# Two transformer layers on 16 items: every engine's order written out, ring tiles chosen per item, fewer identity products

## The reference

```python
# layer 0
h = x + attention(rmsnorm(x), rmsnorm(x), sa_wq, sa_wk, sa_wv, sa_wo)   # 16 heads of 16
h = h + attention(rmsnorm(h), ctx, ca_wq, ca_wk, ca_wv, ca_wo)
h = h + (silu(rmsnorm(h) @ wg) * (rmsnorm(h) @ wu)) @ wd                # 1024 inner
# layer 1
nX, nF = layernorm(ctx, w1, b1), layernorm(h, w2, b2)
att = softmax(nF @ nX.T / 16) @ nX
cross = gelu(att @ fc1_w.T + fc1_b, approximate=False) @ fc2_w.T + fc2_b   # 4 inner
nc = layernorm(cross, w3, b3)
out = nF + gamma2 * (cross + gamma1 * softmax(nc @ nc.T / 16) @ nc)
```

## Time and profile before

| | us |
|---|---|
| median of 3 runs | 936.92 |
| lowest, highest | 936.81, 940.48 |
| the profiled execution: its span, by which it is timed | 938.1 |

### The profile page before, as it was taken

How to read it: one execution, slowest core, us unless ns; L and a number is a source line. 1 busy time by engine, 2 the same in 40 slices (tenths; PEclk the granted TensorE clock), 3 DMA queues, 4 the chain that set the end, 5 groups by cost and what they waited for, 6 DMA issues and landing times.

```text
span 938.1 us, 21220 instructions
## 1 busy us (share of the span) xinstructions
...
## 2 busy tenths in 40 slices
...
GB/s 207 191 148 128 134 76 81 61 105 26 57 101 43 94 64 80 79 81 56 102 38 55 104 44 95 63 81 77 80 55 92 50 43 105 43 33 35 17 12 23
...
## 3 DMA queue, kind: packets, MB, share of 16 engines
...
## 4 chain that ended last, share of the span: by engine, by line
PE 74%; DVE 12%; ACT 6%; issue 3%; DMA 2%; SPq 1%; POOL 1%; ACTq 0%; DVEq 0%
PE mring L1527 21%; PE ring L1527 12%; PE down_ps L1667 9%; PE od L1634 9%; PE ring L1620 7%; PE ring L1600 6%; DVE mx_sa L1296 4%; PE ring L1535 2%; PE mring L1696 1%; PE mring L1769 1%; DVE late_a L1343 1%; ACT probs L1094 1%; PE ring L1607 1%; PE mring L1677 1%; DMA pk_sa<-qkT 1%
## 5 line engine op out<-in xcount | busy, mean ns | idle before, releaser
L1094 ACT ACTIVATE probs<-ring 128x1024 f32<-128x1024 f32 (+1 forms) x192 | 190.9, 1022 | 45.3 <-PE ring L1620 41.5
L849 POOL TENSOR_TENSOR hidT_lo<-late_a,hidT_hi 128x256 fp32r<-128x256 f32 x128 | 95.8, 750 | 316.9 <-ACT hidT_hi L1121 315.7
L1296 DVE TENSOR_REDUCE mx_sa<-ring 128x4 f32<-128x1024 f32 x128 | 153.4, 1215 | 11.4 <-PE ring L1600 11.3
L1301 DVE TENSOR_REDUCE mx_ca<-ring 128x4 f32<-128x308 f32 x128 | 55.1, 474 | 59.8 <-PE ring L1600 59.7
L1349 DVE SCALAR_TENSOR_TENSOR late_a<-late_a,mring 128x256 f32<-128x256 f32 x128 | 52.9, 413 | 49.1 <-ACT late_a L1111 48.7
L1667 PE MATMUL down_ps<-down_hi,hidT_hi 128*128 128x256 f32 x256 | 79.0, 309 | 0.0
L1111 ACT ACTIVATE late_a<-mring 128x256 f32<-128x256 f32 x128 | 48.4, 378 | 51.2 <-PE mring L1527 48.9
L1600 PE MATMUL ring<-pk_sa 63*128 63x256 f32 x512 | 62.8, 329 | 14.9 <-DVE mx_sa L1296 6.4
L1667 PE MATMUL down_ps<-down_lo,hidT_hi 128*128 128x256 f32 x256 | 71.3, 279 | 0.0
L1667 PE MATMUL down_ps<-down_hi,hidT_lo 128*128 128x256 f32 x256 | 71.3, 279 | 0.0
L1121 ACT ACTIVATE hidT_hi<-late_a 128x256 fp32r<-128x256 f32 x128 | 52.6, 413 | 27.0 <-DVE late_a L1351 19.9
...
## 6 DMA issues: line engine op xcount, KB each, us to landing
pk_sa<-qkT SPq DMA_DIRECT2D x96, 256.0 KB, 2.8
qpk_ca<-qkT SPq DMA_DIRECT2D x48, 256.0 KB, 2.6
x_sb<-x SPq DMA_DIRECT2D x16, 256.0 KB, 2.8
x_res<-x SPq DMA_DIRECT2D x16, 256.0 KB, 3.0
out<-o_sb SPq DMA_DIRECT2D x16, 256.0 KB, 2.2
...
```

What stands on the lines that cost most here:

```text
L849: nc.gpsimd.tensor_tensor(hidT[1][:, m % HID, :], hid[:, m % 2, :], hidT[0][:, m % HID, :].bitcast(F32), ALU.subtract).then_inc(S["hidlo"] ...
L1094: nc.scalar.activation(granule(g, tag)[0:rows_, i0:i0 + 2, :, :].rearrange("p i h t -> p h i t"), ring_tile(("E", tag, k))[0:rows_].rearra ...
L1296: nc.vector.tensor_reduce(mx[tag][:, :, :, k].rearrange("p q h -> p h q"), ps[:].rearrange("p h (q t) -> p h q t", t=T), AX_X, ALU.max).th ...
L1301: nc.vector.tensor_reduce(mx[tag][:, :, half, 2 * C * (k % 2) + k // 2:2 * C * (k % 2) + k // 2 + C + 1:C].rearrange("p q i -> p i q"), v, ...
```

## The change

`MOVED` and the sort are gone. `ORDER` now holds each engine's whole list, each word `step@item`; `NAMES` keeps the steps' names in the old sequence, by which the ring tiles are still numbered. Each engine has the same steps for the same items as before, in another order (106 of 204 entries moved on SP, 73 of 276 on POOL, 234 of 1,105 on PE, and so on DVE and ACT). `MOVED_TILES` lists 92 fills, 30 of ring and 62 of mring, which take the other tile, and `tile_at(ring, step, n)` takes the place of `tile_of(ring, step)`. `IDLE` has 66 products at 15 places. The core of the diff:

```diff
 ORDER = {
     "sp": """
-        mr.sa@0 wl.2@11 sk.0@1 sv.0@2 sk.4@-2 vl.ca@-1 ls@8 cl.4@-1 pq.ca@-1 mr.ca@-1 wl.10@-1 sv.4@-3 ldx@2 sk.1@0 cl.1@3 pqk.sa.0@1 wl.4@26 cl.3@0 sv.1@1
+        wl.0@0 wl.1@0 wl.4@0 wl.2@0 wl.6@0 wl.8@0 wl.3@0 wl.7@0 wl.5@0 cl.0@0 wl.9@0 ldx@0 ls@0 ldx@1 lb@0 cl.1@0 pqk.sa.0@0 sv.0@0 cl.2@0 pqk.sa.1@0
...
-MOVED = {
...
-    ("pe", "T.sa"): {0: -2.576471, 1: -0.086275, 4: -0.035294},
...
-}
...
 def sequence(engine):
-    size = len(STEPS[engine])
-    places = []
-    for k, (step, ahead) in enumerate(STEPS[engine]):
-        shifts = MOVED.get((engine, ".".join(map(str, step))), {})
-        for n in range(1 if step[0] in ONCE else B):
-            places.append((n - ahead + (k + 0.5) / size + shifts.get(n, 0), k, step, n))
-    return [(step, n) for _, _, step, n in sorted(places)]
+    words = (word.rsplit("@", 1) for word in ORDER[engine].split())
+    return [(step_of(name), int(n)) for name, n in words]
...
-IDLE = {
-    ("gk.0", 0): 18, ("S.sa.7", 0): 4, ("maxT.sa", 0): 3, ("E.sa.0", 0): 11, ("S.sa.0", 1): 7, ("S.sa.7", 1): 5, ("E.sa.0", 1): 4,
-    ("E.sa.2", 1): 1, ("E.sa.7", 1): 2, ("e2", 13): 5, ("gu.0", 15): 5, ("nFT", 15): 7, ("fT", 14): 3, ("f2", 14): 12, ("s2", 15): 4,
-    ("mT2", 15): 3, ("e2", 15): 2,
-}
+IDLE = {("T.sa", 0): 18, ("gT.0", 0): 4, ("qk.sa", 0): 2, ("S.sa.0", 0): 4, ("S.sa.2", 0): 3, ("S.sa.6", 0): 2, ("E.sa.2", 0): 3, ("nFT", 14): 4, ("s2", 14): 2, ("mT2", 14): 2, ("sc", 15): 3, ("xT", 15): 13, ("mT2", 15): 2, ("u2", 15): 2, ("fT", 15): 2}
...
+MOVED_TILES = {
+    "ring": """
+        T.sa@0 qk.sa@0,1,11 S.sa.2@0 S.sa.3@0,1,4 S.sa.4@0 maxT.sa@0 v.sa@0 E.sa.7@0,15 wo.ca@2,14 S.ca.2@3,4,13 S.ca.3@3,4,13,14 S.ca.1@7 E.sa.5@8
+        S.ca.0@8 E.sa.4@9 wo.sa@14,15 qk.ca@15 maxT.ca@15
+    """,
+    "mring": """
...
+def tile_at(ring, step, n):
+    tiles, _, used = RINGS[ring]
+    return TILES.get((ring, step, n), used.index(step) % tiles)
...
-            tile = used.index(step) % tiles
+            tile = tile_at(ring, step, n)
```

More of the change, by code:

```diff
@@ new lines @@
+        aT.ca@2 norm.mlp@2 h1@3 nXT@1 norm.ca@3 mT2@0 T.mlp@2 v.sa@4 e2@0 gu.0@2 hi.0@2 T.ca@3 norm.sa@5 gu.1@2 maxT.sa@4 qk.ca@3 hi.1@2 gu.2@2
+        E.sa.0@4 E.sa.1@4 gu.3@2 E.sa.2@4 E.sa.3@4 nFT@1 hi.2@2 E.sa.4@4 fT@0 E.sa.5@4 sce@1 hi.3@2 pT@1 E.sa.6@4 T.sa@5 maxT.ca@3 h4@1 gu.4@2
+        E.sa.7@4 qk.sa@5 hi.4@2 gu.5@2 hi.5@2 E.ca.0@3 E.ca.1@3 aT.sa@4 gu.6@2 gu.7@2 E.ca.2@3 E.ca.3@3 xT@1 hi.6@2 hi.7@2 aT.ca@3 norm.mlp@3 h1@4
+        mT2@1 norm.ca@4 nXT@2 v.sa@5 T.mlp@3 e2@1 gu.0@3 hi.0@3 T.ca@4 norm.sa@6 gu.1@3 maxT.sa@5 qk.ca@4 hi.1@3 gu.2@3 E.sa.0@5 E.sa.1@5 gu.3@3
@@ new lines @@
+        qk.sa@10 gu.5@7 hi.4@7 E.ca.0@8 E.ca.1@8 gu.6@7 hi.5@7 aT.sa@9 gu.7@7 E.ca.2@8 E.ca.3@8 hi.6@7 hi.7@7 xT@6 aT.ca@8 norm.mlp@8 h1@9 mT2@6
+        norm.ca@9 v.sa@10 T.mlp@8 nXT@7 e2@6 gu.0@8 hi.0@8 T.ca@9 norm.sa@11 gu.1@8 maxT.sa@10 hi.1@8 qk.ca@9 gu.2@8 E.sa.0@10 E.sa.1@10 gu.3@8
+        E.sa.2@10 E.sa.3@10 nFT@7 E.sa.4@10 hi.2@8 hi.3@8 E.sa.5@10 sce@7 E.sa.6@10 fT@6 T.sa@11 pT@7 gu.4@8 maxT.ca@9 E.sa.7@10 h4@7 hi.4@8 gu.5@8
+        qk.sa@11 E.ca.0@9 E.ca.1@9 hi.5@8 aT.sa@10 gu.6@8 gu.7@8 E.ca.2@9 E.ca.3@9 nXT@8 hi.6@8 hi.7@8 xT@7 aT.ca@9 mT2@7 e2@7 norm.mlp@9 h1@10
@@ new lines @@
+        norm.mlp@13 h1@14 norm.ca@14 nXT@12 v.sa@15 T.mlp@13 mT2@11 e2@11 gu.0@13 hi.0@13 T.ca@14 gu.1@13 maxT.sa@15 hi.1@13 qk.ca@14 gu.2@13
+        E.sa.0@15 E.sa.1@15 gu.3@13 E.sa.2@15 E.sa.3@15 nFT@12 hi.2@13 E.sa.4@15 E.sa.5@15 sce@12 hi.3@13 pT@12 E.sa.6@15 E.sa.7@15 fT@11 gu.4@13
+        maxT.ca@14 gu.5@13 h4@12 hi.4@13 hi.5@13 E.ca.0@14 E.ca.1@14 aT.sa@15 E.ca.2@14 E.ca.3@14 gu.6@13 gu.7@13 hi.6@13 hi.7@13 nXT@13 aT.ca@14
+        xT@12 norm.mlp@14 h1@15 norm.ca@15 mT2@12 T.mlp@14 e2@12 T.ca@15 gu.0@14 gu.1@14 qk.ca@15 hi.0@14 nFT@13 hi.1@14 gu.2@14 gu.3@14 hi.2@14
@@ L81 @@
[L81 to L84 removed]
+        T.sa@0 gT.0@0 qk.sa@0 gv.0@0 gk.0@0 kt@0 gT.1@0 S.sa.0@0 S.sa.1@0 S.sa.2@0 gv.1@0 S.sa.3@0 S.sa.4@0 gT.2@0 S.sa.5@0 S.sa.6@0 S.sa.7@0 gk.1@0
```

417 lines of the change are left out of this document (248 added, 169 removed), and 69 rows, old and new, of the table MOVED.

## The result

| | us |
|---|---|
| changed kernel, median of 4 runs | 949.79 (946.87 to 954.23) |
| kernel before beside it, median of 4 runs | 938.70 (936.81 to 942.75) |
| ratio to before, 95% interval | 1.0123 [1.0084, 1.0161] |
| predicted | 921.5, range 909 to 934 |
| the profiled execution: time, span | 954.23, 952.4 |

The account below looks back on a forecast made before the run. PE was taken to bound the kernel, leaving its idle time, slow clock and switching between kinds of product to gain. Head -10, middle -2 and tail -3.5 sum to -15.5 from 936.9: 921.5 us, range 909 to 934.

Parts of the forecast that it names:

- Head, -10: Start through item 3: earlier query product -4, scores -2.5, exponentials to item 1 -2.5, items 1 to 3 -1 us.
- The 30 identity products fewer are no term by themselves: Identity products dropped from PE: no gain counted, since PE makes them while it would wait; 0.256 us each.
- The terms up to item 1: Head before item 1's first scores: query product -4, item 0's scores -2.5, its exponentials to item 1 -2.5 us.
- The landing at 14.9 us: Head: the context group's load lands at 14.9 us behind 3.5 MB of loads; unhindered it would be 10.4 us.
- Middle, -2: Items 4 to 15: fewer changes of product shape on PE, at most 4.6 us, about half left: -2 us.
- With the neighbour's longer first matmul about 0.1 us is saved for each change of shape left out: Middle: price per change of product shape on PE; 46 fewer changes at 0.1 us give 4.6 us at most.
- The wait that I had named as the bound of the gain: Middle: PE's waits for DVE's maxima around S.sa.4 and v.sa lose part of the saving, leaving about half, -2 us.
- Tail, -3.5: Tail: shorter PE waits at xT@14 -1.7, around T.mlp@15 -1.5, at gu.0@14 -1, against item 14's last steps +0.7 us.
- The +0.7 us for item 14's chain: Tail after dnp.7: the last chain of small steps now also holds item 14's xT to f2, costing 0.7 us.
- The slower one: Rival: each of 41 further fills in a row on one tile costs PE 0.54 us, 22 us together; 945, chance 0.06.
- More: Rival: all shape changes pay (-4.6), head reaches -12, tail loses its low-clock stretches (-8); 912, chance 0.09.
- The head gives half: Rival: PE's clock falls waiting for rows and stays low through item 0's scores; head -5, total 930, chance 0.20.

Follow-up runs that it names:

- c1_head_new: Changed kernel's lists, tiles and identity products up to item 4's first scores, the kernel before behind it; 938.36 us, ratio 1.0008.
- h1_memsets_first: Changed kernel with POOL's memsets of the packed tiles ahead of the first rstd, as in the kernel before; 950.97 us, ratio 1.0103.
- p1_scores_paired: Kernel before with S.sa.4 of items 4 to 14 directly behind S.sa.3 on PE, nXT and mT2 behind both; 941.63 us, ratio 1.0024.
- x2_packing: Changed kernel, on SP: values of items 6 and 7 ahead of packing; items 4 to 15, heads 0 to 7 packed directly before 8 to 15; 942.31 us.
- c2_tail_new: Kernel before up to item 15's first scores, behind it the changed kernel's lists, tiles and identity products; 935.63 us, ratio 0.9955.
- r1_ring_tiles: x2_packing with the 10 moved ring fills of items 4 to 13 back on their old tiles; 947.81 us, ratio 1.0096.

## Why the prediction was wrong

**Head, -10: measured 0.** The step that failed is "The 30 identity products fewer are no term by themselves". It priced them by their own length and asked whether PE would wait there; their other effect is the clock. Without the 19 at item 1 the low clock there is 22.8 to 37.6 us with the new head and 20.5 with the old, with them 3.4 to 13.7 and 0 to 10.2, and that is 2.6 to 4.6 us of the time. The terms up to item 1 were right in sign and too large: 6.8 of 9 us, and less if it is taken against the other profiles with the old head, in which S.sa.0@1 stands at 68.6 to 70.3 and not at 72.2. Against those the head gains 3.2 to 4.9 us up to item 1, so some 4 to 6 of the 9 us were not gained, whatever the clock does behind. The query product came 3.5 us earlier and not 5.8, since I did not look at what POOL's moved memsets do to DVE (with them ahead it was 5.4). The landing at 14.9 us that I worked out for the context group was right (14.66 once nothing else hid it); the rule of the Trainium skill ("DMA: Bandwidth & Descriptors", section "Queues, rings and completion order"), that each SDMA engine consumes a ring's descriptors in order, agrees with the trace, where 10.4 would have gone against it. I priced the packing at its old length: from its last issue to the scores it took 4.54 us for 2.62 (4.3 in c1_head_new and h1_memsets_first, 2.6 in the other profiles with the old head). So the scores gained 1.4 us in these two profiles, and nothing against the 28.7 to 29.3 us of the other profiles with the old head. The large weight loads were over by then: the first of the two rows below, ahead of the packing, has a DMA share of 0.02. A store of values and a context group, issued behind the packing at 25.66 and 26.39 us, fall into the second row; no run shows what they cost.

```profile
20.00:25.00 5.00, 3.91 (x33) 3.74 (x32) 4.22 (x13) 2.77 (x7) 3.19 (x5) 1.00 0.02 8
25.00:29.50 4.50, 2.25 (x19) 1.88 (x17) 0.69 (x1) 4.50 (x15) 4.26 (x7) 1.00 1.01 330
```

**Middle, -2: measured +13.** Two steps failed. "With the neighbour's longer first matmul about 0.1 us is saved for each change of shape left out" read durations that overlap: 0.51 and 0.74 us are lengths of modelled, pipelined matmuls, and the busy time of a whole stretch, the row that counts, is 556.97 us in p1_scores_paired and 556.05 in x2_packing (about 31 of the 46 changes lie in the middle) for 556.38 before and 555.99 in c1_head_new with the same old order. And I read only PE's list there. 9.9 of the 15.3 us lost came from SP's (the values of two items behind a packing, the second half of the heads ahead of the first); the other 5.4 us are waits, most of them on DVE, and why they came stays open. The wait that I had named as the bound of the gain, S.sa.4 and v.sa, gives back all of it, not half: v.sa waits 5.8 us less, S.sa.4 5.3 us and S.sa.6 1.2 us more, and the time is 1.9 us more.

**Tail, -3.5: measured -3.1.** Right in total, and partly by luck in its terms. The wait of 1.74 us at xT@14 is gone, but one of 0.72 us stands inside dnp@15 (-1.0 for -1.7). The 4.55 us at T.mlp@14 and gu.0@14 became three waits of 1.24, 1.48 and 1.59 us in c2_tail_new (-0.2 for -1). Around T.mlp@15 the ten identity products (2.56 us) are gone and the waits are no longer (1.6 for 1.8), -2.8 for -1.5. The +0.7 us for item 14's chain was right: 0.3 to 1.0.

**The rivals.** The slower one ended on the right side by the wrong mechanism: with ten of the moved tiles back the kernel was slower, not faster (r1_ring_tiles). The sum of "More" is -24.6, not -24.8. "The head gives half" had the clock in it, but at item 0, not where the identity products had gone. None of my rivals was a new wait on another engine's queue with the low clock behind it, and 0.06 for slower was too small for an order of 3,351 entries of which I had weighed mainly PE's 1,105.
